# The gate's exponents kept in a PSUM bank, in a fused cross-attention and top-2 mixture kernel

## The reference

```python
x = x + tanh(g_xattn[0]) * xattn(layernorm(x), ctx, Wq, Wkv)       # softmax attention, one head of 512
x = x + tanh(g_ffn[0]) * ffn(layernorm(x), gate_w, gate_b, w1, b1, w2, b2, w3, b3)

def ffn(x, ...):
    logits = einsum('bsd,de->bse', x, gate_w) + gate_b              # 8 experts
    probs = softmax(logits, axis=1)                                # over the 256 tokens of a batch
    vals, idx = top_k(probs, 2)                                    # two experts for each token
    h = relu(x @ w1[e] + b1[e]); h = relu(h @ w2[e] + b2[e]); y = relu(h @ w3[e] + b3[e])
    w_tok, ind = vals and ones, spread to the 8 experts
    v = einsum('ebso,bse->eo', y, w_tok)                           # one vector for each expert
    return einsum('bse,eo->bso', ind, v)
```

## Time and profile before

| | |
|---|---|
| median of 3 runs | 935.58 us (935.42 to 936.04) |
| profiled execution, its own time | 935.88 us |
| its span, first to last instruction | 934.1 us |
| TensorE busy | 906.5 us, 97% |
| VectorE busy | 726.4 us, 78% |
| ScalarE busy | 502.3 us, 54% |
| GpSimd busy | 286.7 us, 31% |
| mean granted TensorE clock | 0.986 of full |

### The profile page before, as it was taken

One profiled execution on the slowest core, in us unless ns is written; L12 is line 12 of the kernel. 1 busy time (PEld: TensorE's weight loads), 2 busy tenths in 40 slices (PEclk: granted clock), 3 DMA queues, 4 the chain that ended last, 5 costly groups with the idle time before them and its releaser, 6 DMA issues.

```text
span 934.1 us, 18566 instructions
## 1 busy us (share of the span) xinstructions
PE 906.5 (97%) x5666; PEld 852.4 (91%) x5666; DVE 726.4 (78%) x1305; ACT 502.3 (54%) x697; POOL 286.7 (31%) x314
## 2 busy tenths in 40 slices
PE   9999999999999999999999999999999999999985
PEld 6989788888888888999999999999999999999971
DVE  5668888888877886977777777777777777777756
ACT  5355444444544458555666666666666666665521
POOL 4234545554545447732111111111111111110003
PEclk9999999999999999999999999999999999999995
DMA  7434443333422264457766888863653754652009
GB/s 238 158 129 141 139 148 120 113 113 112 158 94 89 66 179 115 129 142 199 198 206 153 236 241 244 247 204 108 173 179 109 189 167 113 190 172 59 17 16 360
DMA packets 103239, 143.96 MB, mean 154 GB/s; under 512 B 29600, under 2 KB 68256, under 8 KB 100000
## 3 DMA queue, kind: packets, MB, share of 16 engines
q1 hardware_dynamic: 95776, 126.10, 44.5%
q0 software_dynamic: 7424, 17.38, 7.1%
HBM read 111.91 MB, written 31.53 MB: 154 GB/s over the span
## 4 chain that ended last, share of the span: by engine, by line
PE 75%; POOL 6%; DVE 6%; issue 5%; ACT 4%; SPq 1%; DMA 1%; ACTq 0%; DVEq 0%; POOLq 0%
PE bank L1430 23%; PE bank L1432 23%; PE bank L1431 23%; POOL slot_pair L673 4%; DVE x_all L1420 2%; DVE qa_lo L1008 1%; ACT xn L823 1%; POOL rn L642 1%; POOL rn L659 1%; ACT v_hi L769 1%; DVE probs L1107 1%; POOL rn L657 1%; DMA idx<-slot_pair 0%; DMA wk_raw<-in_wk_t 0%; PE bank L1444 0%
## 5 line engine op out<-in xcount | busy, mean ns | idle before, releaser
L1430 PE MATMUL bank<-h_hi,w_hi 128*128 128x352 f32 x744 | 241.4, 324 | 0.0
L1432 PE MATMUL bank<-h_hi,w_lo 128*128 128x352 f32 x744 | 240.1, 323 | 0.0
L1431 PE MATMUL bank<-h_lo,w_hi 128*128 128x352 f32 x744 | 239.0, 321 | 0.0
L703 POOL DMA_INDIRECT xg<-xn_dram,idx x72 | 88.2, 1224 | 363.1 <-DMA idx<-slot_pair 347.8
L1008 DVE TENSOR_TENSOR w_lo<-w_raw,w_hi 128x2048 fp32r<-128x2048 f32 (+1 forms) x74 | 165.1, 2231 | 28.7 <-ACT w_hi L880 18.6
L897 ACT ACTIVATE h<-bank,bias 128x352 f32<-128x352 f32 x192 | 96.0, 552 | 139.1 <-PE bank L1432 110.1
L880 ACT ACTIVATE w_hi<-w_raw 128x2048 fp32r<-128x2048 f32 x71 | 135.5, 1908 | 36.0 <-PE bank L1432 32.8
L1008 DVE TENSOR_TENSOR h_lo<-h,h_hi 128x704 fp32r<-128x704 f32 x88 | 78.1, 888 | 79.8 <-ACT h_hi L903 78.2
L1430 PEld LDWEIGHTS bank<-h_hi,w_hi 128*128 128x128 f32 x744 | 139.8, 188 | 0.1
L1431 PEld LDWEIGHTS bank<-h_lo,w_hi 128*128 128x128 f32 x744 | 139.7, 188 | 0.0
L1432 PEld LDWEIGHTS bank<-h_hi,w_lo 128*128 128x128 f32 x744 | 139.3, 187 | 0.0
(11 more groups left out here) (221 smaller groups left out, 1757.2 us busy)
## 6 DMA issues: line engine op xcount, KB each, us to landing
w_raw<-in_w SPq DMA_DIRECT2D x24, 1024.0 KB
xq<-rows_dram SPq DMA_DIRECT2D x80, 176.0 KB
w_raw<-in_w SPq DMA_DIRECT2D x48, 256.0 KB
rows_dram<-xg SPq DMA_DIRECT2D x20, 512.0 KB, 3.3
wb<-slot_pair SPq DMA_DIRECT2D x24, 352.0 KB
xt_raw<-in_x_t SPq DMA_DIRECT2D x16, 512.0 KB, 3.9
c_raw<-in_ctx_t SPq DMA_DIRECT2D x16, 512.0 KB
x_all<-in_x SPq DMA_DIRECT2D x16, 512.0 KB, 4.8
```

Source lines behind the costliest of these rows:

```text
L703: pool.indirect_dma_start(xg[0:n, c], None, rows, bass.IndirectOffsetOnAxis(ap=idx[0:n, c, 0:1], axis=0)).then_inc(gathered, 16)
L1430: pe.matmul(out_ap, lh, rh, start=(i == 0), stop=False)
L1431: pe.matmul(out_ap, lh, rl, start=False, stop=False)
L1432: last = pe.matmul(out_ap, ll, rh, start=False, stop=(i == n - 1))
```

## The change

ScalarE writes the exponentials over the logits' own place in PSUM, `R_LOGIT`, and VectorE's multiplication reads them there. The SBUF buffer `gexp` is dropped, so the line numbers behind it are one lower in the changed kernel (1107 is 1106, 814 is 813, 1575 is 1574).

```diff
--- before.py
+++ after.py
@@ -234,7 +234,6 @@
             logit_low = alloc(ph, "logit_low", [E, S], F32)
             logit = alloc(ph, "logit", [E, S], F32)
             gmax = alloc(ph, "gmax", [E, 1], F32)
-            gexp = alloc(ph, "gexp", [E, S], F32)
             gsum = alloc(ph, "gsum", [E, 2], F32)
             probs = alloc(ph, "probs", [E, S], F32)
 
@@ -811,7 +810,7 @@
 
             def gate_exp(m):
                 need(act, gmax_ready, m + 1)
-                act.activation(gexp[:], logit[:], ACT.Exp, bias=gmax[:, 0:1], accum_out=gsum[:, 0:1]
+                act.activation(R_LOGIT, logit[:], ACT.Exp, bias=gmax[:, 0:1], accum_out=gsum[:, 0:1]
                                ).then_inc(gexp_done, 1)
 
             def norm2(m):
@@ -1104,7 +1103,7 @@
                 dve.wait_ge(gexp_done, m + 1)
                 dve.reciprocal(gsum[:, 1:2], gsum[:, 0:1]).then_inc(gate_step, 1)
                 dve.wait_ge(gate_step, 2 * m + 2)
-                dve.tensor_scalar(probs[:], gexp[:], gsum[:, 1:2], None, ALU.mult).then_inc(probs_ready, 1)
+                dve.tensor_scalar(probs[:], R_LOGIT, gsum[:, 1:2], None, ALU.mult).then_inc(probs_ready, 1)
 
             def attended(m):
```

## The result

The changed kernel takes 927.1 us (median of 3 runs, 925.24 to 928.15), the kernel before 935.58. The ratio is 0.9901, 95% interval 0.9887 to 0.9916: faster by 8.5 us, forecast 9.2. All 12 timed runs of the changed kernel in this study lie between 925.05 and 928.49, their median is 927.0. The profiled execution is its fastest of the first three, 925.24 us.

What follows compares the result with a forecast made beforehand. TensorE was taken to bound the kernel, with one recurring wait for `probs`. 8.4 + 0.56 - 0.24 + 0.56 = 9.3 us off 935.88 gave 926.6, against the median 926.3; forecast 926.4, range 925.2 to 928.8.

Steps and rivals of the forecast that it cites:

- The bound and the cause: Attention stage: TensorE sets the pace, waiting nine times, 8.9 us, for `probs`, which is held until GpSimd's `c_lo` ends.
- The prices: Gate: `probs` reading PSUM takes 0.41 us in place of up to 1.92; the Exp writing PSUM stays at 0.49.
- the chain: GpSimd's sends and `rn`, then `xn`, `v_hi`, `pt_hi`, `c_hi`, `gexp`, ending in `probs`: 18.82 or 19.10 us per batch.
- its margin: Regular batches: TensorE's own 19.3 us is longer than the chain through the other engines by 0.2 to 0.5 us.
- The regular batches: Transposes of the gate's probabilities: eight waits for `probs` go, 8.4 us; 19.3 us from one to the next.
- the pipeline terms: At the transposes: beginning in the pipeline's shadow adds 8 x 0.07 = 0.56 us; the first matmul behind costs 0.24.
- The end of the stage: Between 250 and 371 us, all TensorE waits for follows from its own earlier results, so the rest moves as a block.
- The wait at 371.10: Ninth wait, last batch: `probs` at 0.41 us in place of 1.33 removes it, 0.49 + 0.07 = 0.56 us.
- The expert stage: From 400 to 900 us TensorE is busy throughout at full clock, so the gain reaches the end.
- The first (the chain takes over): Attention stage: GpSimd's sends or `c_lo` come later, or `probs` takes 0.6 us or more; 927 to 931 us; chance 0.06.
- The second (the PSUM form is held too): `probs` out of PSUM is still held by GpSimd, stays at 1.9 us; 935.6 us; chance 0.04.
- The third: Behind the transposes, `oh` and `ind`, with two SBUF sources, are held by `c_lo` and `ranks` waits; about 940; chance 0.03.

Runs made afterwards that it cites:

- The first two experiments: Kernel before, with GpSimd's `c_lo` cut into four instructions: 927.75 us; kernel before, with an accumulator added to VectorE's SBUF-to-SBUF `probs`: 926.93 us.
- ScalarE's half: Changed kernel, but VectorE multiplies the SBUF tile `logit`; the exponents still go to PSUM: 184.89 us from first to tenth transposes, against 184.94 before.
- the experiment: Changed kernel with ScalarE's Exp moved ahead of `c_hi` in batches 0 to 10, so that `c_lo` comes later: 930.6 us, ratio 0.9950.

## Why the prediction was right

**The bound and the cause.** TensorE as the engine to watch, `probs` as its one recurring wait, GpSimd's `c_lo` as what holds `probs`: all three stand. The first two experiments show the third: cut the GpSimd instruction or change the form of VectorE's, and the long hold is gone, with the operands where they were.

**The prices.** `probs` was put at 0.41 us and takes 0.47; the rows chosen as nearest (a cast and a two-source sum) are other operations. The Exp was put at no change and takes 0.04 us less. The two errors cancel in the chain to 0.02 us, by luck. Nothing in the result hangs on either, as TensorE is the later one: `probs` ends 0.28 us ahead of the transposes in one kind of batch and 0.61 in the other, 0.15 of which pass in any case. That slack of 0.13 us is half of what the prediction read (19.35 against 19.10), so its margin was thinner than it said.

**The regular batches.** The eight waits with the pipeline terms were put at 8.4 + 0.56 - 0.24 = 8.7 us. From the first to the tenth transposes the three profiles of the changed kernel give 176.12, 176.43 and 250.85 - 74.47 = 176.38 us against 184.94: 8.5 to 8.8. The 0.3 us between them are one wait of TensorE, for `xn` near 244 us: 0.66 in the first, 0.93 and 0.94 in the others. The 19.3 us per batch came as 19.36.

**The end of the stage.** The wait at 371.10 was put at 0.56 us and is gone in all profiles. But I had argued that all that TensorE waits for there follows from its own earlier results, and this step was wrong: one link hangs on the landing of a DMA, and on which of VectorE's `w_lo` the sends behind it meet. From the tenth to the sixteenth transposes the three profiles take 109.85, 111.05 and 362.00 - 250.85 = 111.15 us against 111.41: a gain of 1.6 in one and of 0.3 to 0.4 in two, where 0.56 was forecast. The wait for `et_lo`, 1.0 us before, was 1.1, 2.4 and 2.4, which is the difference between the three. I had not counted it.

The other way, two waits of the kernel before are gone that I had not counted either. The first, with what stands ahead of it on VectorE:

```profile
330.69 0.69 DVE L1016 TENSOR_REDUCE smax<-bank 128x2 f32<-128x512 f32 x1 [2.07 <-remote]
...
332.85 0.18 PE L1502 MATMUL bank<-ind,tri_half 128*128 128x16 bf16 x1 [0.37 <-DVE ind L1143]
```

VectorE stood idle for 2.07 us for something that the profile doesn't name, and from batch 13's transposes to batch 14's it took 345.18 - 327.88 = 17.30 us. In the ten other profiles of this study it is 16.76 or 16.77, also in the one of ScalarE's half, where `probs` is held as before. So this half microsecond belongs to the one execution of the kernel before that was profiled, and the change did not win it. The second is a wait of 0.39 us for `h_lo` at 353.23. ScalarE's `h` had started 5.15 us behind the transposes of batch 14, and 4.34 or 4.35 in the ten others, so this is most likely of the same sort. I don't know the cause of either. So where two of the three profiles come out near the 0.56 of the forecast, it is luck: the waits that the profile before happened to have and the longer wait for `et_lo` work against each other. Even the wait at 371.10 isn't in every execution with a held `probs`: in the profile of ScalarE's half the last `probs` took 0.47 us, and TensorE didn't wait.

Whether this wait and the granted clock behind it also make the rest of the spread of 3 us between runs stays open, as unprofiled runs show no waits.

**The expert stage** passed the gain on whole: 563.0 us from the last transposes to the end in both.

**The rivals.** The first (the chain takes over) was close: 0.13 to 0.15 us of slack in every second batch, and a second multiplication uses it up. The second (the PSUM form is held too) did not happen. The third did not happen, and the experiment shows both that its mechanism is real and that 0.42 us of room keep it away.

## What to carry to other kernels

Look at the spread of a small instruction's durations before its mean: here one size took 0.34 us in one batch and 1.92 in another because it was held, and its end laid beside the other engines' ends said by whom. Between VectorE and GpSimd several remedies are equal (a PSUM source, a form with an accumulator, shorter GpSimd instructions); choose the one that costs the least elsewhere. Then work out who is late next and by how much: here 0.15 us for the chain, 0.4 us for `oh`, and a reordering of two steps on ScalarE or on GpSimd, each harmless to look at, gave back 4.0 and 4.5 us. And before a wait is booked as a cost of a kernel, look for it in a second profile: of the waits at the end of this stage, one half microsecond stood in a single profile of eleven.

## What the hardware showed beyond that

ScalarE's Exp on 8x256 is faster into PSUM than into SBUF, 454 against 493 ns. VectorE's multiplication of that size takes 0.34 us from SBUF, 0.47 from PSUM, and 0.47 from SBUF with an accumulator. An instruction with two SBUF sources is held by GpSimd's too (0.51 in place of 0.19 us for `oh` in the kernel with the Exp ahead of `c_hi`, ending 0.04 us after `c_lo`). One with a source in PSUM and one in SBUF is not: `qa_lo` takes 0.67 us beside `c_lo` in the changed kernel. And the hold comes from DMA work of GpSimd as well: in the kernel before, the `probs` at 289.24 took 0.57 us and ended at 289.81, 0.09 us after one of GpSimd's sends (288.76, 0.96 us long), and the one at 343.65 took 0.44 and ended 0.09 us after a gather (343.07, 0.93).

The hold goes the other way too. GpSimd's sends and gathers that start inside a `w_lo` of VectorE's (two SBUF sources) take up to 3.06 us in place of about 1 and end 0.83 to 0.86 us behind it in the rows above.
